# Graph network on one core: PSUM banks shared by several sums, later adds, and more rooms for gathered rows, planes and one-hots

## The chip, the cores and the metric

The kernel runs on one core of a Trainium2 chip. The metric is the device time of one launch in microseconds (us). TensorE (PE) does matrix products into PSUM, VectorE (DVE) and ScalarE (ACT) work element by element, GpSimd (POOL) issues the gathers by index, SyncE (SP) issues the plain transfers.

## What is computed

A graph of 6250 nodes with 128 features has 106250 edges (50000 drawn ones, each in both directions, and 6250 loops). Four networks follow one another, each with a residual and a layer norm:

```
x = layernorm(x + L0(x, edges, edge_attr))       # edge MLP, segment sum, GRU cell
x = layernorm(x + relu(conv(x)))                 # L1: normalised by degrees
x = layernorm(x + prelu(conv(x)))                # L2
h = relu(conv_w(x, W1)); h = relu(conv_w(h, W2)) # L3: weighted edges, 128 -> 256 -> 256
x = layernorm(x + conv_w(h, W3))                 #     -> 128

def _gcn_conv(x, W, b, src, dst, norm, n_nodes):
    m = x @ W
    msg = m[src] * norm[:, None]
    out = jax.ops.segment_sum(msg, dst, num_segments=n_nodes)
    return out + b
```

The change concerns the five products of a sparse 6250 x 6250 matrix with the rows of all nodes that L1, L2 and L3 need. They are the kernel's layers `l1`, `l2`, `l3a`, `l3b`, `l3c`. Layer `l3b` has rows of 256 features where the others have 128, as its product is taken between two weight matrices.

## The kernel before, in words

The first 2200 us (of the profile) run the edge network and the GRU cell and build the matrices in DRAM: blocks of 128 x 128 of counts (`counts_fwd`, `counts_rev`, for l1 and l2) or of weights (`weights_fwd`, for l3a to l3c). Nothing there changes.

`layer()` then makes each product in two ways at once. **Dense part:** the 49 node blocks form 13 groups of four. For most groups SP brings the group's matrix in seven chunks of 7 source blocks (`mat_...`, `slots` chunk slots), and PE multiplies every source block by it (L1469, out to `po_...`, four accumulators in PSUM). A little after its last chunk a group is taken: DVE adds what was left out (L1718) and for some groups a low sum (L1723), PE multiplies by the layer's weights (L1501 to L1523), and DVE and ACT finish the rows. The rows that fitted no block (the rest) come by one gather, L1376, and small matmuls L1417 and L1421 at the start of each layer.

**Low part:** the edges into the first few groups aren't multiplied as blocks. They are sorted by destination, and 69 *half steps* (103 in l3b) of four tiles of 128 edges each are woven into the dense part, so many to a chunk (`beside`), placed between the source blocks of a chunk. Half step j takes:

- POOL, `rows_of_step`: four gathers of 128 rows (L1390) into room j of a ring of `RL` rooms.
- DVE, `low_hots`: a one-hot of each edge's destination within 64 nodes (L1667), `HL` rooms, `HL - 1` half steps ahead.
- In l3a to l3c the rows are float32 and are made into three bfloat16 planes: ACT `high` (L1577, four operations, with the edge's weight), DVE `off_high` (L1675, four), ACT `mid` (L1583), DVE `last_plane` (L1681). There are two split rooms, so `high(j)` waits for PE's half step j-2. In l1 and l2 the table already has three planes.
- PE, the half step (L1440): 12 matmuls of 128 x 64 (24 in l3b) into one bank of PSUM.
- DVE, `add_sums` (L1690): that bank is added into `acc_...` at a place that is read from `low_first`.

The order is written out. At a chunk, DVE does for each of its half steps j: one-hots of j+3 (j+1 in l3b), `off_high(j+1)`, `add_sums(j)`, `last_plane(j+1)`. PE waits before half step j for its planes or rows, its one-hots, and for the bank:

```
if j >= pas:
    pe.wait_ge(added, j - pas + 1)
```

`pas` is the number of banks: 3, and 1 in l3b, which has only the bank `pl_l3b` for this. The rings lie in parts of the two large arrays `rows_a` and `rows_b` that a layer leaves free (`spare_of`), four rooms each and three in l3b.

Of the kernel before, what the change touches and what calls it, by code (L numbers as in the profile page):

```python
# [20 lines left out]
P = 128  # L21
N = 6250
E = 106250
FD = 128
# [8 lines left out]
TH = 4  # L33
# [88 lines left out]
def build(nc, a, out):  # L122
    with ExitStack() as ctx:
# [1050 lines left out]
        def layer(name, kind, K, Fo, given, mats, self_n, dis_in, bias, dis_out, wts, table, table_out, made, stored, slots,  # L1174
                  lows, spare):
# [16 lines left out]
            low_groups = list(range(low_n // GB))  # L1192

# [29 lines left out]
            if both:  # L1223
                for n, g in begun:
                    assert g * GB >= low_n or sum(len(js) for js in beside[:n]) >= min(low_js, PER_GROUP * g + LATE_BY)
            if not both:
                free = [p * CHKS + at for p in range(1, len(products) + 1) for at in LATER]
                for q in low_groups:
                    at = next(n for n in free if sum(len(js) for js in beside[:n]) >= min(low_js, PER_GROUP * q + LATE_BY))
                    free = [n for n in free if n > at]  # L1230
                    begun.append((at, q))
# [11 lines left out]
            RL = 3 if two else 4  # L1243
            HL = 2 if two else 4
            pas = 1 if two else 3

            with ExitStack() as c:
# [15 lines left out]
                room = spare[:, 0:RL * TH * wide] if exact else spare[:, 0:RL * TH * row_n // 2].bitcast(BF16)  # L1263
                ring = room.rearrange("p (q t f) -> p q t f", q=RL, t=TH)
                hot = sb(f"hot_{name}", [P, HL, TH, W], BF16, c)

                split = sb(f"split_{name}", [P, 2, 3, TH, wide], BF16, c) if exact else None
                rec_t = sb(f"rec_{name}", [P, 8], F32, c)
                near = sb(f"near_{name}", [P, 2], F32, c)
# [15 lines left out]
                pa = pl[:].unsqueeze(1) if two else ps(f"pa_{name}", [P, pas, 512], c)  # L1285
# [35 lines left out]
                def is_low(g):  # L1321

                    return g * GB < low_n

# [14 lines left out]
                with nc.Block() as block:  # L1339
# [25 lines left out]
                    def _(pool):  # L1365
# [19 lines left out]
                        def rows_of_step(j):  # L1385
# [3 lines left out]
                            for t in range(TH):  # L1389
                                pool.indirect_dma_start(  # L1390
                                    ring[:, j % RL, t, :], None, table,
# [12 lines left out]
                    def _(pe):  # L1404
# [23 lines left out]
                        def half_step(j):  # L1428
# [5 lines left out]
                            if j >= pas:  # L1434
                                pe.wait_ge(added, j - pas + 1)
                            for k in range(K):
                                for t in range(TH):
                                    for v in range(3):
                                        rows = split[:, j % 2, v, t, k * P:(k + 1) * P] if exact else ring[:, j % RL, t, v * P:(v + 1) * P]
                                        mm = nc.tensor.matmul(pa[:, j % pas, k * W:(k + 1) * W], rows, hot[:, j % HL, t, :],  # L1440
# [106 lines left out]
                    def _(act):  # L1547
# [23 lines left out]
                        def high(j):  # L1571

                            act.wait_ge(gathered[j % RL], 16 * TH * (j // RL + 1))
                            if j >= 2:
                                act.wait_ge(step_sum, j - 1)
                            for t in range(TH):
                                part = nc.scalar.activation(split[:, j % 2, 0, t, :], ring[:, j % RL, t, :], ACT.Copy,  # L1577
# [329 lines left out]
```

## Time and profile before

| | |
|---|---|
| runs of the kernel before | 4619.05 us median of 3 (4617.8 to 4621.76) |
| span of the one profiled execution | 5156.7 us |
| of it: up to layer l1 | 0 to 2200 |
| l1 | 2200 to 2778, 578 us |
| l2 | 2778 to 3250, 472 us |
| l3a | 3250 to 3771, 521 us |
| l3b | 3771 to 4637, 866 us |
| l3c | 4637 to 5157, 520 us |

No other time of the profiled execution is recorded than its span, which is 537.6 us longer than the median. Times within the profile are read against the span. In its rows the share in the last columns of a window is the granted clock of TensorE, then the share of DMA time and the rate; a value in square brackets in a timeline is the engine's idle time just before the row and what ended it.

### The profile page before, as it was taken

What the parts mean: (1) busy time and instruction counts of PE and PEld (TensorE: products, weight loads), DVE (VectorE), ACT (ScalarE), POOL (GpSimd) and SP (SyncE); (2) the same over time, 40 slices, a digit from 0 to 9 for tenths busy, and PEclk for the clock granted to TensorE, in tenths of its full rate; (3) what the DMA queues carried; (4) which work ended last, traced back from release to release, by engine and by line L of the source; (5) the groups of instructions that cost most, each with busy time, mean ns of one, the idle gap of its engine ahead of it and who ended that gap; (6) DMA issues with size and microseconds to landing.
All of it is one profiled execution on the core that took longest, in us unless ns stands there. A gap on an engine that the chain in (4) does not pass through costs nothing. (4 is left out here: it accounts for less than half of the span.)

```text
span 5156.7 us, 82749 instructions
## 1 busy us (share of the span) xinstructions
PE 4030.2 (78%) x30748; PEld 2679.0 (52%) x30767; DVE 3057.5 (59%) x6135; ACT 1489.2 (29%) x3024; POOL 2773.1 (54%) x2361
## 2 busy tenths in 40 slices
PE   2788788788888853268887888688978888887888
PEld 2677677677777743234443444344444554544344
DVE  5888777777787785835553233355435555522554
ACT  0333455455555531200000000122214433412332
POOL 3676666766776600046663665366436655605663
PEclk6777888898888876679998888799989999998999
DMA  4344566566666642079995666577745545537776
GB/s 148 116 125 131 183 194 201 182 213 198 198 204 199 206 137 81 29 253 318 318 325 173 196 204 191 188 274 276 284 149 187 184 159 182 179 115 246 267 264 232
DMA packets 611991, 1019.31 MB, mean 198 GB/s; under 512 B 90372, under 2 KB 417056, under 8 KB 611208
## 3 DMA queue, kind: packets, MB, share of 16 engines
q1 hardware_dynamic: 475788, 773.72, 44.0%
q0 software_dynamic: 90848, 199.74, 13.3%
q10 hardware_dynamic: 44956, 40.55, 2.4%
q8 instruction: 247, 4.05, 0.3%
q14 instruction: 152, 1.25, 0.1%
HBM read 736.98 MB, written 276.75 MB: 197 GB/s over the span
## 5 line engine op out<-in xcount | busy, mean ns | idle before, releaser
L871 POOL DMA_INDIRECT x<-p_table,src_i x832 | 1180.3, 1419 | 625.1 <-DVE x L610 338.3
L1390 POOL DMA_INDIRECT rows_b<-x_table,low_src x552 | 577.3, 1046 | 660.5 <-POOLq L140 309.8
L1390 POOL DMA_INDIRECT rows_a<-h_table,low_src x412 | 449.8, 1092 | 298.8 <-DVE split_l3b L1681 176.6
L1469 PE MATMUL po_l3b<-mat_l3b,rows_b 128*128 128x512 f32 (+1 forms) x1372 | 583.6, 573 | 29.0 <-DMA mat_l3b<-weights_fwd 20.6
L853 ACT CAST st_cnt<-ps_mat 128x512 bf16<-128x512 f32 (+1 forms) x825 | 445.4, 586 | 510.4 <-PE ps_deg L768 244.0
L783 PE MATMUL ps_mat<-rows_a,hot_s 128*128 128x128 bf16 x4851 | 406.2, 241 | 98.8 <-issue 68.4
L1469 PE MATMUL po_l3a<-mat_l3a,rows_a 128*128 128x512 f32 (+1 forms) x882 | 393.7, 593 | 46.6 <-DMA mat_l3a<-weights_fwd 32.1
L1469 PE MATMUL po_l3c<-mat_l3c,rows_a 128*128 128x512 f32 (+1 forms) x882 | 391.8, 591 | 28.1 <-DMA mat_l3c<-weights_fwd 19.3
L783 PEld LDWEIGHTS ps_mat<-rows_a,hot_s 128*128 128x128 bf16 x4851 | 327.1, 109 | 144.7 <-issue 88.6
L1469 PEld LDWEIGHTS po_l3b<-mat_l3b,rows_b 128*128 128x128 f32 x1372 | 250.4, 203 | 256.0 <-issue 233.5
L1469 PE MATMUL po_l<-mat_l,rows_b 128*128 128x512 bf16 (+1 forms) x1323 | 323.4, 394 | 64.5 <-issue 43.9
L1390 POOL DMA_INDIRECT rows_a<-x_table,low_src x276 | 281.2, 1019 | 168.6 <-issue 86.8
L1390 POOL DMA_INDIRECT rows_a<-m_table,low_src x276 | 277.2, 1004 | 170.2 <-issue 91.5
L1469 PE MATMUL po_l<-mat_l,rows_a 128*128 128x512 bf16 (+1 forms) x1323 | 296.7, 381 | 91.0 <-DVE mat_l L1709 70.4
L598 DVE TENSOR_TENSOR rows_a<-rows_a,slots 128x1792 bf16<-128x1792 bf16 (+1 forms) x198 | 366.7, 1885 | 1.4
L763 PE MATMUL ps_mat<-rows_a,hot_s 128*128 128x128 bf16 x1617 | 269.2, 232 | 110.3 <-ACT st_cnt L853 43.0
L766 PE MATMUL ps_mat<-hot_s,rows_a 128*128 128x256 bf16 x1225 | 338.2, 296 | 3.9 <-issue 3.9
L764 PE MATMUL ps_deg<-slots,hot_s 128*128 128x1 bf16 x2401 | 295.1, 172 | 50.3 <-issue 32.3
L858 ACT COPY st_wt<-ps_mat 128x512 f32<-128x512 f32 (+1 forms) x429 | 246.0, 573 | 159.8 <-PE ps_deg L768 59.7
L1624 ACT ACTIVATE t_l<-y_l 128x512 f32<-128x512 f32 (+1 forms) x26 | 15.7, 605 | 956.0 <-DVE y_l L1764 591.6
L793 PE MATMUL pm<-w1eT,rows_a 65*128 65x128 f32 x1664 | 270.1, 313 | 5.4 <-DVE x L610 4.6
L1469 PEld LDWEIGHTS po_l3a<-mat_l3a,rows_a 128*128 128x128 f32 x882 | 165.8, 206 | 201.9 <-issue 166.5
(407 smaller groups left out, 7488.0 us busy)
## 6 DMA issues: line engine op xcount, KB each, us to landing
weights_fwd<-st_wt SPq DMA_DIRECT2D x396, 256.0 KB
mat_l<-counts_fwd SPq DMA_DIRECT2D x112, 896.0 KB
mat_l3a<-weights_fwd SPq DMA_DIRECT2D x56, 1792.0 KB
mat_l3c<-weights_fwd SPq DMA_DIRECT2D x56, 1792.0 KB
counts_rev<-st_cnt SPq DMA_DIRECT2D x588, 128.0 KB
rev_l<-counts_rev SPq DMA_DIRECT2D x84, 896.0 KB
mat_l3b<-weights_fwd SPq DMA_DIRECT2D x42, 1792.0 KB
counts_fwd<-st_cnt SPq DMA_DIRECT2D x396, 128.0 KB
```

The lines of the kernel that those rows point to most:

```text
L598: V.tensor_tensor(hot_w[:, h, v, 0:n, :], hot_d[:, h, 0:n, :], per_row(slots[:, u % 2, 2 + v, ks], P), ALU.mult).then_inc(hots_ready, 1)
L763: nc.tensor.matmul(ps_mat[:, b, q * P:(q + 1) * P], half, rows, start=True, stop=True)
L764: nc.tensor.matmul(ps_deg[:, 2 * k + q:2 * k + q + 1], half, slots[:, u % 2, NV, k:k + 1], start=False, stop=False)
L766: nc.tensor.matmul(ps_mat[:, b, rev_at:rev_at + len(halves) * P], rows, hot_s[:, h, j0 + j, 0:len(halves) * P], start=True, stop=True)
L783: mm = nc.tensor.matmul(ps_mat[:, f % 3, (2 * j + q) * P:(2 * j + q + 1) * P], half, hot_w[:, h, v, j0 + j, :], start=(v == 0), stop=(v == 2))
L793: mm = nc.tensor.matmul(pm[:, j % 2, t * FD:(t + 1) * FD], edge[:, i % 2, (h * TH + t) * P:(h * TH + t + 1) * P], w1eT[:], start=True, sto ...
L853: nc.scalar.copy(st_cnt[:, q, :, j * 2 * P:j * 2 * P + n_col], ps_mat[:, f % 3, :].rearrange("p (d c) -> p d c", d=2)[:, :, 0:n_col]).then ...
L858: nc.scalar.copy(to, ps_mat[:, f % 3, 0:w]).then_inc(evicted, 1)
L871: pool.indirect_dma_start(ring[:, j % RING, t * FD:(t + 1) * FD], None, p_table, bass.IndirectOffsetOnAxis(src_i[:, j * TH + t:j * TH + t ...
L1390: pool.indirect_dma_start(ring[:, j % RL, t, :], None, table, bass.IndirectOffsetOnAxis(low_src[:, j * TH + t:j * TH + t + 1].bitcast(U32), 0)
L1469: mm = nc.tensor.matmul(po[:, p % 2, k, 0:nb * P].rearrange("p (d c) -> p d c", c=P), rows[:, s, k * P:(k + 1) * P], cols, start=(s == 0 a ...
L1624: nc.scalar.activation(t1[:, 0:nb, 0:FD], y2[:, f % ys, 0:nb], ACT.Square).then_inc(act_out, 1)
```

## The change

- **Banks.** In l1, l2, l3a and l3c the three banks hold two sums each (`SUMS` = 2, side by side in a bank). In l3b the one bank holds four. PE waits for adds only at the first sum of a bank, and then until all sums that lay in it are added; DVE adds a bank's sums only once its last sum is made (`in_full`).
- **Adds.** They come later in DVE's order: at half step j all adds up to j+1-`LAG` (3, and 1 in l3b), by whole banks, so in pairs, and in fours in l3b. The take of a low group first brings the adds up to what it needs (`needed`), and the chunk at which a low group may begin follows from that: the end of group 1 moves from chunk 33 to 38 in l3a and l3c, that of group 4 in l3b from 38 to 40.
- **Rooms.** One-hots: 8 rooms for 4, 3 for 2 in l3b, made as many half steps ahead as before. Ring: 8 for 4 in l2, 6 for 4 in l3a and l3c, as before in l1 (4) and l3b (3). Split rooms: 5 for 2 in l3c, 2 elsewhere. Chunk slots: 6 for 3 in l2. The small tile `near` now lies in `small`.

```diff
+            BANKS, SUMS, LAG = (1, 4, 1) if two else (3, 2, 3)
+            def in_full(j):
+                return min(low_js, -(-j // SUMS) * SUMS)
+            def needed(g):
+                return in_full(PER_GROUP * g + LATE_BY)
...
-            RL = 3 if two else 4
-            HL = 2 if two else 4
-            pas = 1 if two else 3
+            RL = len(ring_rooms)
+            HL, HOTS_AHEAD = (3, 1) if two else (8, 3)
+            SPLITS = 2 if two else 2 + len(split_rooms)
...
+                def sum_room(j):
+                    return pa[:, j // SUMS % BANKS, j % SUMS * K * W:(j % SUMS + 1) * K * W]
...
-                            if j >= pas:
-                                pe.wait_ge(added, j - pas + 1)
+                            if j % SUMS == 0 and j >= BANKS * SUMS:
+                                pe.wait_ge(added, j - BANKS * SUMS + SUMS)
+                            to = sum_room(j)
...
-                            if j >= 2:
-                                act.wait_ge(step_sum, j - 1)
+                            if j >= SPLITS:
+                                act.wait_ge(step_sum, j - SPLITS + 1)
...
+                        def add_until(end):
+                            while begun_adds[0] < end and in_full(begun_adds[0] + 1) <= end:
+                                add_sums(begun_adds[0])
+                                begun_adds[0] += 1
                         def add_sums(j):
...
-                            dve.wait_ge(step_sum, j + 1)
+                            dve.wait_ge(step_sum, in_full(j + 1))
...
                             g = tasks[f]
                             nb = blocks_in(g)
+                            if is_low(g):
+                                add_until(needed(g))
...
-                                if j + HL - 1 < low_js:
-                                    low_hots(j + HL - 1)
+                                if j + HOTS_AHEAD < low_js:
+                                    low_hots(j + HOTS_AHEAD)
                                 if exact and j + 1 < low_js:
                                     off_high(j + 1)
-                                add_sums(j)
+                                add_until(j + 1 - LAG)
                                 if exact and j + 1 < low_js:
                                     last_plane(j + 1)
...
-              tables[1], tables[2], rows_of(rows_a, FD), rows_of(rows_a, FD), 3, 0, spare_b)
+              tables[1], tables[2], rows_of(rows_a, FD), rows_of(rows_a, FD), 6, 0,
+              rooms_of(rows_b, a_end, b_end, step_planes) + rooms_of(rows_a, NP, a_end, step_planes), [])
...
-              m_table, None, None, None, 3, 0, spare_a)
+              m_table, None, None, None, 3, 0, rooms_of(rows_a, NP, a_end, step_rows),
+              rooms_of(rows_b, 0, 3 * step_planes, step_planes))
```

DVE in l3b, near the layer's start, before: from one-hots to one-hots is a half step, and each has its add (the three rows ahead of an add read where it goes).

```order
L1675 SCALAR_TENSOR_TENSOR rows_a<-rows_a,low_weight,split_l3b 128x256 x4
L1685 TENSOR_LOAD low_first
L1685 ISA x2
L1690 ISA
L1690 TENSOR_TENSOR acc_l3b<-acc_l3b,pl_l3b 128x2x64
L1681 TENSOR_TENSOR split_l3b<-rows_a,split_l3b 128x1024
L1667 TENSOR_TENSOR hot_l3b<-iota_row,low_local 128x256
L1675 SCALAR_TENSOR_TENSOR rows_a<-rows_a,low_weight,split_l3b 128x256 x4
```

The same engine and place after the change (L1683 is the one-hots, L1691 the subtractions, L1697 the last plane, L1712 the add).

```order
L1697 TENSOR_TENSOR split_l3b<-rows_a,split_l3b 128x1024
L1683 TENSOR_TENSOR hot_l3b<-iota_row,low_local 128x256
L1691 SCALAR_TENSOR_TENSOR rows_a<-rows_a,low_weight,split_l3b 128x256 x4
L1707 TENSOR_LOAD low_first
L1707 ISA x2
L1712 ISA
L1712 TENSOR_TENSOR acc_l3b<-acc_l3b,pl_l3b 128x2x64
L1707 TENSOR_LOAD low_first
L1707 ISA x2
L1712 ISA
L1712 TENSOR_TENSOR acc_l3b<-acc_l3b,pl_l3b 128x2x64
L1707 TENSOR_LOAD low_first
```

The four rows of an add stand four times in a row there, ahead of the last plane; the three half steps before have none.

POOL at the start of l2, before: the gathers of four half steps, then the loop's registers, then the rest's gather.

```order
L1390 DMA rows_b<-x_table,low_src 128x384 x16
L1341 TENSOR_LOAD left_i
L1341 ISA x2
L1342 TENSOR_LOAD left_i
L1342 ISA x2
L118 UNCONDITIONAL_BRANCH x2
L96 ISA
L1376 DMA sums_l<-x_table,rec_l 128x384
```

After (L1404 is the ring's gather, L1390 now the rest's):

```order
L1404 DMA rows_b<-x_table,low_src 128x384 x16
L1404 DMA rows_a<-x_table,low_src 128x384 x16
L1341 TENSOR_LOAD left_i
L1341 ISA x2
L1342 TENSOR_LOAD left_i
L1342 ISA x2
L118 UNCONDITIONAL_BRANCH x2
L96 ISA
L1390 DMA sums_l<-x_table,rec_l 128x384
```

The gathers of four more half steps, into rooms in the other array, stand ahead of the rest's gather.

## Rows read from the trace of the kernel before

**Rows 1.** The page's head.

```profile
span 5156.7 us, 82749 instructions
```

**Rows 2.** Windows by stage (3a, 3b, 3c): busy times, clock, DMA share, GB/s.

```profile
3250.00:3771.00 521.00, 440.99 (x1912) 226.59 (x1912) 231.10 (x569) 127.85 (x345) 282.17 (x277) 0.92 0.73 258
3771.00:4637.00 866.00, 755.61 (x4538) 434.76 (x4538) 434.59 (x815) 292.97 (x541) 450.72 (x413) 0.94 0.50 167
4637.00:5157.00 520.00, 425.60 (x1863) 211.89 (x1863) 242.31 (x647) 138.52 (x371) 278.18 (x277) 0.92 0.72 252
```

**Rows 3.** Groups by line and form, 3b: busy us, mean ns, idle before, releasers.

```profile
L1390 POOL DMA_INDIRECT rows_a<-h_table,low_src x412 | 449.8, 1092 | 298.8 <-DVE split_l3b L1681 176.6 <-issue 122.2
...
L1577 ACT ACTIVATE split_l3b<-rows_a,low_weight 128x256 bf16<-128x256 f32 x412 | 175.5, 496 | 268.6 <-DMA rows_a<-h_table,low_src 99.7 <-PE pl_l3b L1440 86.4 <-DMA rows_a<-x_table,low_src 73.5
...
L1681 DVE TENSOR_TENSOR split_l3b<-rows_a,split_l3b 128x1024 bf16<-128x1024 f32 x103 | 125.8, 1222 | 41.2 <-ACT split_l3b L1583 33.7 <-issue 7.4
...
L1440 PE MATMUL pl_l3b<-hot_l3b,split_l3b 128*128 128x64 bf16 x2472 | 91.5, 195 | 47.9 <-DVE split_l3b L1681 39.5 <-issue 8.1
...
L1690 DVE TENSOR_TENSOR acc_l3b<-acc_l3b,pl_l3b 128x128 f32 x103 | 29.4, 286 | 244.1 <-PE pl_l3b L1440 131.2 <-DMA rows_a<-x_table,low_src 112.8
...
L1718 DVE TENSOR_TENSOR sums_l3b<-po_l3b,left_l3b 128x1024 f32<-128x1024 f32 x12 | 14.7, 1221 | 45.0 <-PE po_l3b L1488 43.2 <-DMA rev_l<-counts_rev 1.8
```

**Rows 4.** Timeline of a half step in 3b: start, duration, engine, line, operation.

```profile
4035.68 0.86 PE L1440 MATMUL pl_l3b<-hot_l3b,split_l3b 128*128 128x64 bf16 x24 [0.47 <-issue]
...
4037.41 0.28 DVE L1690 TENSOR_TENSOR acc_l3b<-acc_l3b,pl_l3b 128x128 f32 x1
4037.53 1.04 ACT L1583 CAST split_l3b<-rows_a 128x1024 bf16<-128x1024 f32 x1 [1.78 <-DVE rows_a L1675]
...
4038.48 1.70 ACT L1577 ACTIVATE split_l3b<-rows_a,low_weight 128x256 bf16<-128x256 f32 x4
4038.60 1.23 DVE L1681 TENSOR_TENSOR split_l3b<-rows_a,split_l3b 128x1024 bf16<-128x1024 f32 x1 [0.91 <-ACT split_l3b L1583]
...
4039.93 0.86 PE L1440 MATMUL pl_l3b<-hot_l3b,split_l3b 128*128 128x64 bf16 x24
4040.21 1.67 DVE L1675 SCALAR_TENSOR_TENSOR rows_a<-rows_a,low_weight,split_l3b 128x256 f32<-128x256 f32 x4
```

**Rows 5.** Timeline of two adds close together, layer two.

```profile
2971.10 0.22 DVE L1690 TENSOR_TENSOR acc_l<-acc_l,pa_l 128x64 f32 x1 [3.52 <-DMA x<-p_table,src_i]
...
2971.96 0.22 DVE L1690 TENSOR_TENSOR acc_l<-acc_l,pa_l 128x64 f32 x1 [0.30 <-issue]
```

**Rows 6.** Timeline of a half step in 3c and what follows it.

```profile
4988.64 0.51 PE L1440 MATMUL pa_l3c<-hot_l3c,split_l3c 128*128 128x64 bf16 x12 [0.24 <-issue]
...
4998.40 0.40 ACT L1577 ACTIVATE split_l3c<-rows_a,low_weight 128x128 bf16<-128x128 f32 x1 [7.69 <-DMA rec_l3b<-left_rec]
...
4999.43 0.80 PE L1440 MATMUL pa_l3c<-hot_l3c,split_l3c 128*128 128x64 bf16 x12 [4.61 <-issue]
```

**Rows 7.** Windows of the same place.

```profile
4990.00:4998.80 8.80, 4.83 (x15) 2.03 (x13) 0.35 (x3) 1.02 (x3) 4.71 (x5) 1.00 0.41 143
4998.80:5002.20 3.40, 2.77 (x15) 1.76 (x16) 2.80 (x9) 2.19 (x7) 1.03 (x1) 0.50 0.80 243
```

**Rows 8.** Groups by line: PE's half steps in 3a and 3c, POOL's gathers in 3c.

```profile
L1440 PE MATMUL pa_l3a<-hot_l3a,split_l3a 128*128 128x64 bf16 x828 | 36.5, 195 | 37.5 <-issue 37.5
...
L1390 POOL DMA_INDIRECT rows_a<-m_table,low_src x276 | 277.2, 1004 | 170.2 <-issue 91.5 <-DVE split_l3c L1681 78.6
...
L1440 PE MATMUL pa_l3c<-hot_l3c,split_l3c 128*128 128x64 bf16 x828 | 37.4, 197 | 55.0 <-issue 55.0
```

**Rows 9.** Timeline of POOL at the start of 3c, after its first 20 gathers.

```profile
4692.41 1.17 POOL L1390 DMA_INDIRECT rows_a<-m_table,low_src  x1 [17.94 <-DVE split_l3c L1681]
```

**Rows 10.** Timeline of layer two's start: the rest's gather and PE's first rest matmuls.

```profile
2799.03 0.94 POOL L1376 DMA_INDIRECT sums_l<-x_table,rec_l  x1 [0.30 <-issue]
...
2812.25 0.48 PE L1421 MATMUL pl_l<-zero 128*128 128x128 f32 x2 [0.15 <-remote]
```

More of the change, by code:

```diff
@@ L1224, in layer @@
                 for n, g in begun:
-                    assert g * GB >= low_n or sum(len(js) for js in beside[:n]) >= min(low_js, PER_GROUP * g + LATE_BY)
+                    assert g * GB >= low_n or sum(len(js) for js in beside[:n]) >= needed(g)
             if not both:
@@ L1228, in layer @@
                 for q in low_groups:
-                    at = next(n for n in free if sum(len(js) for js in beside[:n]) >= min(low_js, PER_GROUP * q + LATE_BY))
+                    at = next(n for n in free if sum(len(js) for js in beside[:n]) >= needed(q))
                     free = [n for n in free if n > at]
@@ L1262, in layer @@
                 acc = sb(f"acc_{name}", [P, K, span + W], F32, c)
-                room = spare[:, 0:RL * TH * wide] if exact else spare[:, 0:RL * TH * row_n // 2].bitcast(BF16)
-                ring = room.rearrange("p (q t f) -> p q t f", q=RL, t=TH)
+                ring = [(room if exact else room.bitcast(BF16)).rearrange("p (t f) -> p t f", t=TH) for room in ring_rooms]
                 hot = sb(f"hot_{name}", [P, HL, TH, W], BF16, c)
-                split = sb(f"split_{name}", [P, 2, 3, TH, wide], BF16, c) if exact else None
+                split = [sb(f"split{q}_{name}", [P, 3, TH, wide], BF16, c)[:] for q in range(2)] if exact else []
+                split += [room.bitcast(BF16).rearrange("p (v t f) -> p v t f", v=3, t=TH) for room in split_rooms]
                 rec_t = sb(f"rec_{name}", [P, 8], F32, c)
-                near = sb(f"near_{name}", [P, 2], F32, c)
+                near = small[:, 0, 0:2]
                 kinds = 2 if both else 1
@@ L1283, in layer @@
                 pl = ps(f"pl_{name}", [P, 512], c)
-                pa = pl[:].unsqueeze(1) if two else ps(f"pa_{name}", [P, pas, 512], c)
+                pa = pl[:].unsqueeze(1) if two else ps(f"pa_{name}", [P, BANKS, 512], c)
                 mat_in = [sem(f"mat_in_{name}{q}") for q in range(slots)]
@@ L1438, in half_step @@
                                     for v in range(3):
[L1439 to L1440 removed]
+                                        rows = split[j % SPLITS][:, v, t, k * P:(k + 1) * P] if exact else ring[j % RL][:, t, v * P:(v + 1) * P]
+                                        mm = nc.tensor.matmul(to[:, k * W:(k + 1) * W], rows, hot[:, j % HL, t, :],
                                                               start=(t == 0 and v == 0), stop=(t == TH - 1 and v == 2))
@@ L1582, in mid @@
                             act.wait_ge(high_off, j + 1)
-                            nc.scalar.copy(split[:, j % 2, 1], ring[:, j % RL]).then_inc(mid_ready, 1)
+                            nc.scalar.copy(split[j % SPLITS][:, 1], ring[j % RL]).then_inc(mid_ready, 1)
                         def store(f):
@@ L1727, in take @@
                                 dve.wait_ge(taken, f + 1)
-                                dve.wait_ge(added, sum(len(js) for js in beside[:starts[f]]))
+                                dve.wait_ge(added, begun_adds[0])
                                 end = at + nb * P
@@ L1797, in _ @@
                         chain.step(V.memset(acc[:], 0.0))
-                        for j in range(HL - 1):
+                        for j in range(HOTS_AHEAD):
                             low_hots(j)
```

31 lines of the change are left out of this document (17 added, 14 removed).

## The prediction

> **What bounds the kernel now.** I read the page's head first: a span of 5156.7 us [rows 1]. The one profiled execution is 537.6 us (11.6%) longer than the median of the runs, 4619.05 us, so the sum below is made as a difference against the profiled execution and then added to the median. Terms that are chains of instruction durations carry over as they are; terms that are waits may belong to the profiled execution alone, and that doubt is a rival below. 0.2% (9 us) is about what a measurement of this kernel can tell from no change.
>
> The windows by stage [rows 2] come next. TensorE is busy for 441 of 521 us in 3a, 756 of 866 in 3b and 426 of 520 in 3c, and the DMA engines for 0.73, 0.50 and 0.72 of these stretches. So 3b goes by TensorE's program alone, and each microsecond that PE waits there is one of the kernel; 3a and 3c go by PE too, with the transfers close behind. Layer one keeps its rooms and chunk slots.
>
> In 3b the groups [rows 3] give most prices of a half step's parts: four gathers on POOL at 1.092 us, four high planes on ACT at 0.496, a last plane on DVE at 1.222 and an add at 0.286. PE idles 47.9 us before its 2472 small matmuls (103 half steps of 24), 39.5 of it for the last plane. The timeline of one half step after another [rows 4] shows the loop: PE ends half step j-1 at 4036.54; ACT's mid plane (1.04 us) ends at 4038.57 and the next high planes run 1.70 us from 4038.48; DVE's last plane from 4038.60 lets PE start half step j at 4039.93; and DVE's subtractions for j+1 start only at 4040.21 and take 1.67. The add of half step j-1 stood at 4037.41, **ahead** of all that.
>
> **3b: the add that PE waits for moves behind a step.** Before, the add of half step j-1 comes in DVE's step j-1, and PE's half step j waits for it; it is done 2.2 us early in the timeline. Now four sums lie in the one bank. The order shows three DVE steps without adds, then four adds in the step of j *behind* the subtractions of j+1, and PE's half step j (j a multiple of 4) waits for all four. DVE can't reach them sooner: the subtractions of j+1 wait for the high planes of j+1, and those for PE's half step j-1, since 3b still has two split rooms. From the end of PE's half step j-1: 0.3 us until ACT is through with the mid plane (ACT and DVE have caught up in the stall four steps before; in the timeline, with no such stall, it is 1.94), 1.70 for the high planes, 1.67 for the subtractions, then four adds. Two adds in a row stand 0.86 us apart and one lasts 0.22 there, 0.28 in 3b [rows 5, 4]: 3 x 0.86 + 0.28 = 2.86. Together 6.5, with hand-overs 6.6 us. PE's own work between half steps two source blocks apart is 3.39 us (4036.54 to 4039.93), so 5.1 for three and 6.8 for four. PE's order has 25 such waits: 16 at two blocks, 6 at three, 3 at four. Stalls: 16 x 3.2 = 51 and 6 x 1.5 = 9. Four of the waits lie in a chunk that also takes a group, where DVE has L1718 (1.221), L1723 of the same shape and a diagonal of half its width ahead: 4 x 3 = 12. **+72.** Upper end: 1.94 in place of 0.3 at 22 places, +36 more. Lower end: adds back to back at 0.28, 1.7 less at 22 places, -38.
>
> **The clock.** In 3c, after PE had stood for 4.61 us [rows 6], its granted clock was 0.50 for 3.4 us where it had been 1.00 [rows 7]: the lower of its two levels, 1.2 GHz; half speed for 3.4 us costs 1.7. The new stalls are shorter than that one. I take it for 20 of them and for 0.7 of these: **+24** (0 to 43, all 25).
>
> **3b, gain.** Three steps of four lose their add. Of the 47.9 us before half steps I take **-15** (0 to -48). The third one-hot room is worth 0: the last plane is the wait's releaser, not the one-hots, whose cover is that they are written a step ahead.
>
> **3a and 3c: six ring rooms for four, three banks of two sums for three of one, and in 3c five split rooms for two.** PE idles 37.5 and 55.0 us before their half steps, with no releaser named [rows 8]. More rooms let POOL and ACT run on while DVE is busy with a group's end, and at the layers' start: in 3c POOL stands 17.94 us once its rooms are full [rows 9]. But POOL is idle for 170.2 us of 3c in all, so gathers aren't late on the whole, and PE has dense matmuls to fill the time. I take a third of 92.5: **-30**. Ends: 0, and -120, all of the waits with a clock term of 1.7 at some 16 of them. The end of group 1 moves from chunk 33 to 38 in both, and group 4's in 3b from 38 to 40; the dense work between covers that: 0.
>
> **Layer two: eight ring rooms for four, six chunk slots for three.** POOL's order has 32 gathers ahead of the one at L1376 which the rest's sums need, where it had 16. L1376 starts at 2799.03, and 16 more gathers at 0.94 + 0.30 us put it at 2819; PE takes up the rest's sums at 2812.25 [rows 10]. PE would stand some 8 us, of which steps gathered sooner and more chunk slots give part back: **+5** (-10 to +20). Layer one: 0 (-10 to 0).
>
> **Sum:** +72 +24 -15 -30 +5 = +56, so 4619 + 56 = **4675 us**. This case's own range is 4637 (the adds at their lower end) to 4730 (the chain at its upper end, 36, and the clock at 43).
>
> **A rule that speaks against the sum.** In one place of 3c [rows 6] PE's half step ends at 4989.15, and ACT, whose high planes wait for it, starts at 4998.40 after 7.69 us idle. No full room explains that: PE had the only missing signal. So I count most of the 92.5 us as waits of the profiled execution. The Trainium skill (Trainium Kernel Development and Optimization, Best Practices) says that consistent bubbles can mean that SBUF or PSUM space has run out. By that rule the idle time before half steps is what this change removes, and the sum would be the first rival's. The same notes (Perfetto Trace Analysis, on an instruction's lifecycle) say that a semaphore update isn't part of the instruction's row; no run here shows yet how long one takes without the profiler.
>
> **Rivals.**
> *Full rooms were the limit (22%).* The idle before half steps is real in plain runs. For it: 37.5, 55.0 and 47.9 us stand before the same line in all three layers, and in 3c POOL does stop with its rooms full. Against it: [rows 6]. 0.8 x 92.5 goes (-74), the clock after 20 such stalls (-34), 3b's 47.9 goes (-48), and 3b's new stalls stay (+96): -60, **4559 us**.
> *Gathers set 3b's pace (14%).* Four gathers with their gaps are 4 x (1.092 + 0.30) = 5.57 us a half step, more than 3.39. If PE waits for gathers in a run of near half steps anyway, the stall is only 6.6 - 5.6 = 1.0 at 22 places and the takes' 12: +34, no clock term. The starts of 3a and 3c give 2 x 17.9 = 36 and their waits 10, 3b 15, layer two costs 5: -22, **4597 us**. Against it: group and timeline name the last plane, not a gather.
> *Little happens (8%).* The four adds are reached in time and the rooms were never short: **4612 to 4619 us**. Against it: the order puts the adds behind subtractions that can't start earlier.
> *The forecast (56%)* is the slower side's one mechanism. It decides as soon as the path from half step j-1 to the fourth add, 6.6 us, is longer than PE's work between.
>
> **How the numbers follow.** The forecast's 56 give 54 slower and 2 same; the first rival's 22 give 21 faster and 1 same; the second's 14 give 10, 2, and 2 slower; the third's 8 give 1, 6 and 1. Faster 0.32, same 0.11, slower 0.57. The range, 4575 to 4730, leaves out most of the first rival's lower part and the forecast's worst clock term.
>
> **What would show it.** Four adds in a row in 3b, about 0.86 us apart, and PE idle some 3 us before each fourth half step, ended by DVE's add; 3b 60 to 100 us longer than 866; more of 3b at 0.50 of the clock; 3a and 3c shorter by 10 to 20 us each; L1376's successor in layer two some 20 us behind the first gathers' end. It is wrong if the fourth add ends before PE arrives, or if 3b is no longer than before, or if the idle time before half steps in 3a and 3c is gone and the runs are faster by as much.

## The result, and the profile after

| | us |
|---|---|
| kernel before | 4620.41, median of 4 (4617.8 to 4626.03) |
| changed kernel | 4664.75, median of 4 (4659.21 to 4670.83) |
| ratio | 1.0096, 95% interval 1.0078 to 1.0114 |
| forecast | 4675, range 4575 to 4730 |

The change costs 44 us, 0.96%. That is slower, as forecast, and 10 us from the number. How its terms came out is told below.

First something without which no profile here can be read: the profile of before and the times above don't belong together. The changed kernel's profiled execution has a span of 4669.0 us and belongs to a run of 4670.83 us, where the profiled execution of before had 5156.7 [rows 1]. In the experiments the kernel before, unchanged, took 5169.8, 5169.88, 5109.26, 5112.47 and 5112.93 us on five chips, and 4620.07 on a sixth. So **chips come in two kinds** for this kernel, here called the quicker and the slower kind. (No chip was seen in both kinds. That each stays in its kind isn't shown.) By its span and its stages the profile of before is one of the slower kind; both medians of the result are of the quicker kind. The prediction took the difference for waits that belong to the profiled execution alone. They don't: on the slower kind profiled executions of the kernel before took 5168.13 and 5180.66 us, as long as the others there.

So the rows of before are answered below by two pages: the changed kernel, and the experiment h1, which on a quicker chip took 4625.75 us beside 4620.07 of the kernel before (ratio 1.0011, 0.9995 to 1.0028). h1 has 3b as before, the ring, split rooms and chunk slots of before, and elsewhere pairs of sums added in their own step. It stands in for the kernel before, of which no profile on a quicker chip exists and from which its time can't be told. Two things of the change are in h1 too and so in no difference below: the extra rooms for one-hots, and the pairs with the later start of group 1.

Windows by stage of h1 (layer two, 3a, 3b, 3c): length, busy times of PE, PEld, DVE, ACT, POOL, then clock, DMA share, GB/s.

```profile
2539.60:2937.90 398.30, 326.32 (x2354) 177.00 (x2354) 155.85 (x355) 10.53 (x26) 271.82 (x277) 0.93 0.69 219
2937.90:3389.50 451.60, 420.18 (x1912) 218.12 (x1912) 232.58 (x569) 128.68 (x345) 280.81 (x277) 0.97 0.84 297
3389.50:4192.90 803.40, 732.39 (x4538) 421.08 (x4538) 438.64 (x816) 291.22 (x541) 446.23 (x413) 0.97 0.53 180
4192.90:4625.60 432.70, 403.99 (x1863) 204.60 (x1863) 243.76 (x647) 139.27 (x371) 278.38 (x277) 0.97 0.86 303
```

The same windows of the changed kernel.

```profile
2546.70:2943.70 397.00, 322.37 (x2354) 176.59 (x2354) 154.96 (x355) 10.53 (x26) 272.79 (x277) 0.92 0.70 219
2943.70:3388.80 445.10, 419.52 (x1912) 219.37 (x1912) 234.49 (x569) 128.81 (x345) 281.44 (x277) 0.97 0.86 302
3388.80:4240.00 851.20, 749.65 (x4538) 426.30 (x4538) 443.09 (x815) 291.78 (x541) 433.67 (x413) 0.95 0.51 170
4240.00:4669.00 429.00, 402.67 (x1863) 205.38 (x1863) 245.45 (x647) 138.28 (x371) 278.18 (x277) 0.97 0.87 305
```

3b is 47.8 us longer. Layer two, 3a and 3c are 1.3, 6.5 and 3.7 us shorter, and layer one 3.0 (568.2 and 565.2). The layers together make +33; the other 10 us between the two spans lie before layer one (1971 and 1982 us), where the two programs are the same. That stretch scatters by itself: four executions on one chip of the slower kind took 2209 to 2239 us for it (f0 to f4 below).

What PE's idle time before half steps and before turns in 3b became, first in h1 and then in the changed kernel (groups by line and form; L1455 is the half step, L1528 the turn).

```profile
L1455 PE MATMUL pl_l3b<-hot_l3b,split_l3b 128*128 128x64 bf16 x2472 | 90.0, 194 | 22.5 <-issue 11.3 <-DVE split_l3b L1697 11.0
...
L1528 PE MATMUL pc_l3b<-ident,y_l3b 128*128 128x128 f32 x98 | 16.1, 315 | 31.0 <-DVE y_l3b L1776 31.0
```

```profile
L1455 PE MATMUL pl_l3b<-hot_l3b,split_l3b 128*128 128x64 bf16 x2472 | 94.1, 197 | 66.4 <-DVE acc_l3b L1712 62.8 <-DVE split_l3b L1697 3.5
...
L1528 PE MATMUL pc_l3b<-ident,y_l3b 128*128 128x128 f32 x98 | 14.2, 290 | 15.2 <-DVE y_l3b L1776 15.2
```

PE now waits 62.8 us for the add, a wait that did not exist. In return the 22.5 us for planes became 3.5, and the turns' 31.0 became 15.2: time that PE stands is time in which ACT and DVE catch up. In all, PE is idle for 101.6 us of 3b where h1 has 71.0 (a window's length less PE's busy time), 30.6 more. PE's busy time rose by 17.3 us (732.39 to 749.65) over the same 4538 instructions. 30.6 + 17.3 are the 47.8 us. The 17.3 go with the clock (0.97 to 0.95): by the clock's own records in the two traces, 3b of the changed kernel has 90.1 us at 0.50 and h1's has 49.0. The 41 us more at half speed would cost 20.5, an estimate, near the 17.3.

One stall, in the timeline of the changed kernel.

```profile
3451.73 0.86 PE L1455 MATMUL pl_l3b<-hot_l3b,split_l3b 128*128 128x64 bf16 x24
...
3452.87 1.70 ACT L1592 ACTIVATE split_l3b<-rows_a,low_weight 128x256 bf16<-128x256 f32 x4
...
3454.61 1.67 DVE L1691 SCALAR_TENSOR_TENSOR rows_a<-rows_a,low_weight,split_l3b 128x256 f32<-128x256 f32 x4
...
3456.19 0.71 DVE L1712 TENSOR_TENSOR acc_l3b<-acc_l3b,pl_l3b 128x128 f32 x2
...
3457.44 0.29 DVE L1712 TENSOR_TENSOR acc_l3b<-acc_l3b,pl_l3b 128x128 f32 x1 [0.54 <-DVE acc_l3b L1712]
...
3458.26 0.29 DVE L1712 TENSOR_TENSOR acc_l3b<-acc_l3b,pl_l3b 128x128 f32 x1 [0.53 <-DVE acc_l3b L1712]
...
3458.69 0.86 PE L1455 MATMUL pl_l3b<-hot_l3b,split_l3b 128*128 128x64 bf16 x24 [2.58 <-DVE acc_l3b L1712]
```

It is the loop of [rows 4] with the add moved. PE's half step ends at 3452.59, the high planes start 0.28 us later, the subtractions follow, and four adds end at 3458.55. PE stood 2.58 us. Windows of the changed kernel in and after that stall:

```profile
3456.00:3458.60 2.60, 0.11 (x1) 0.00 (x0) 1.40 (x6) 1.04 (x1) 1.89 (x2) 1.00 0.35 101
3459.70:3463.10 3.40, 3.40 (x6) 1.41 (x5) 1.99 (x5) 1.66 (x5) 2.78 (x3) 0.50 0.52 154
```

The granted clock falls to 0.50, the lower level, for 3.4 us after 2.6 us of an idle PE, as it did after a longer stop in [rows 7]. Not every wait has this behind it. Of the 20 waits for the add, 14 were followed by a stretch at 0.50, of 3.4 or 6.8 us. Of the ten that lasted 2.4 to 2.8 us, seven were. A wait of 3.35 us that ended at 4133.94 was not, as the window behind it shows:

```profile
4134.00:4140.00 6.00, 6.00 (x59) 3.50 (x60) 3.52 (x7) 2.75 (x5) 0.00 (x0) 1.00 0.05 5
```

3a and 3c after the change: PE's half steps (in 3c some planes lie in `rows_b`), which answer [rows 8].

```profile
L1455 PE MATMUL pa_l3a<-hot_l3a,split_l3a 128*128 128x64 bf16 x828 | 35.4, 193 | 0.2 <-issue 0.2
...
L1455 PE MATMUL pa_l3c<-hot_l3c,rows_b 128*128 128x64 bf16 x492 | 21.0, 193 | 0.2 <-issue 0.2
```

The 37.5 and 55.0 us of [rows 8] are gone. But on h1, on a quicker chip with the rooms of before, they are 5.9 and 4.4 us already:

```profile
L1455 PE MATMUL pa_l3a<-hot_l3a,split_l3a 128*128 128x64 bf16 x828 | 35.4, 193 | 5.9 <-DVE split_l3a L1697 4.4 <-issue 1.5
...
L1455 PE MATMUL pa_l3c<-hot_l3c,split_l3c 128*128 128x64 bf16 x828 | 35.4, 193 | 4.4 <-DVE split_l3c L1697 3.2 <-issue 1.2
```

Layer two: PE's wait for the rest's gather in h1 (sixteen gathers ahead) and PE's waits in its half steps.

```profile
L1455 PE MATMUL pa_l<-hot_l,rows_b 128*128 128x64 bf16 x828 | 36.3, 195 | 36.0 <-DMA rows_b<-x_table,low_src 16.2 <-issue 15.7 <-DVE hot_l L1683 4.0
...
L1431 PE MATMUL pl_l<-sums_l 128*128 128x128 bf16 x3 | 0.5, 304 | 9.7 <-DMA x<-p_table,src_i 9.7
```

The same in the changed kernel (thirty-two ahead; half steps from either array).

```profile
L1455 PE MATMUL pa_l<-hot_l,rows_b 128*128 128x64 bf16 x432 | 18.7, 194 | 9.7 <-issue 4.1 <-DMA rows_b<-x_table,low_src 2.8 <-DVE hot_l L1683 2.8
...
L1455 PE MATMUL pa_l<-hot_l,rows_a 128*128 128x64 bf16 x396 | 17.3, 195 | 10.3 <-DMA rows_a<-x_table,low_src 7.1 <-issue 3.2
...
L1431 PE MATMUL pl_l<-sums_l 128*128 128x128 bf16 x3 | 0.5, 305 | 28.7 <-remote 28.7
```

The wait for the rest's gather, which POOL now issues 40.2 us after its first (2587.06 and 2546.86), grew from 9.7 to 28.7 us, and half steps wait 20.0 us in place of 36.0. A new wait took the place of the ones removed. The six chunk slots changed little: PE's waits for the matrix are 17.9 us where h1 has 18.8.

### The profile page after: what moved, and what is told of

Its sections match the earlier page's. It is cut to its first block and busy times, and to the rows that moved or that the text cites. A ratio compares the mean times of both kernels' runs of the same rounds, so it can differ in the third digit from the quotient of the medians.

```text
span 4669.0 us, 82757 instructions
## 1 busy us (share of the span) xinstructions
PE 3827.6 (82%) x30767; PEld 2568.0 (55%) x30767; DVE 3072.3 (66%) x6135; ACT 1470.4 (31%) x3024; POOL 2802.3 (60%) x2361
## 3 DMA queue, kind: packets, MB, share of 16 engines
q14 instruction: 152, 1.25, 0.1%
## 5 line engine op out<-in xcount | busy, mean ns | idle before, releaser
L871 POOL DMA_INDIRECT x<-p_table,src_i x832 | 1214.4, 1460 | 398.3 <-issue 234.2
L1404 POOL DMA_INDIRECT rows_b<-x_table,low_src x420 | 460.0, 1095 | 538.8 <-POOLq L140 310.8
L1404 POOL DMA_INDIRECT rows_a<-h_table,low_src x412 | 432.7, 1050 | 299.0 <-DVE split_l3b L1697 180.4
L1484 PE MATMUL po_l3b<-mat_l3b,rows_b 128*128 128x512 f32 (+1 forms) x1372 | 586.9, 576 | 21.4 <-DMA mat_l3b<-weights_fwd 20.5
L1404 POOL DMA_INDIRECT rows_a<-x_table,low_src x408 | 410.6, 1006 | 127.9 <-issue 122.8
L1484 PE MATMUL po_l3a<-mat_l3a,rows_a 128*128 128x512 f32 (+1 forms) x882 | 376.5, 574 | 30.9 <-DMA mat_l3a<-weights_fwd 30.1
L783 PE MATMUL ps_mat<-rows_a,hot_s 128*128 128x128 bf16 x4851 | 360.6, 226 | 9.5
L1404 POOL DMA_INDIRECT rows_a<-m_table,low_src x276 | 277.2, 1004 | 87.7 <-issue 85.6
L763 PE MATMUL ps_mat<-rows_a,hot_s 128*128 128x128 bf16 x1617 | 254.7, 224 | 85.2 <-DVE rows_a L598 61.6
L766 PE MATMUL ps_mat<-hot_s,rows_a 128*128 128x256 bf16 x1225 | 321.2, 283 | 0.0
L783 PEld LDWEIGHTS ps_mat<-rows_a,hot_s 128*128 128x128 bf16 x4851 | 291.2, 101 | 48.0 <-ACT st_wt L858 37.9
L1484 PE MATMUL po_l<-mat_l,rows_b 128*128 128x512 bf16 (+1 forms) x1323 | 285.9, 371 | 18.7 <-DMA mat_l<-counts_fwd 17.9
L1639 ACT ACTIVATE t_l<-y_l 128x512 f32<-128x512 f32 (+1 forms) x26 | 15.7, 605 | 899.5 <-DVE y_l L1788 891.6
L1691 DVE SCALAR_TENSOR_TENSOR rows_a<-rows_a,low_weight,split_l3b 128x256 f32<-128x256 f32 x412 | 172.7, 481 | 156.0 <-ACT split_l3b L1592 154.4
```

The lines of the kernel that those rows point to most:

```text
L763: nc.tensor.matmul(ps_mat[:, b, q * P:(q + 1) * P], half, rows, start=True, stop=True)
L766: nc.tensor.matmul(ps_mat[:, b, rev_at:rev_at + len(halves) * P], rows, hot_s[:, h, j0 + j, 0:len(halves) * P], start=True, stop=True)
L783: mm = nc.tensor.matmul(ps_mat[:, f % 3, (2 * j + q) * P:(2 * j + q + 1) * P], half, hot_w[:, h, v, j0 + j, :], start=(v == 0), stop=(v == 2))
L871: pool.indirect_dma_start(ring[:, j % RING, t * FD:(t + 1) * FD], None, p_table, bass.IndirectOffsetOnAxis(src_i[:, j * TH + t:j * TH + t ...
L1404: pool.indirect_dma_start(ring[j % RL][:, t, :], None, table, bass.IndirectOffsetOnAxis(low_src[:, j * TH + t:j * TH + t + 1].bitcast(U32), 0)
L1484: mm = nc.tensor.matmul(po[:, p % 2, k, 0:nb * P].rearrange("p (d c) -> p d c", c=P), rows[:, s, k * P:(k + 1) * P], cols, start=(s == 0 a ...
```

## The experiments

Theory A is the prediction's: 3b's four adds behind the next step's subtractions cost the time, the rest moves little. Theory B: the waits of the first profile are real limits of the kernel, and 3b's stall only replaces them.

**e0, f0: the kernel before, again** (two chips, both of the slower kind). No edit.

> The kernel before, unchanged, for a second profile beside the changed kernel's, whose span (4669.0 us) is no longer than its runs. Theory A (3b's adds cost, rooms gain a little): the span comes out near 4620; 3b near 775 us where the changed kernel has 851, 3a and 3c some 455 and 440 (445 and 429 changed), PE hardly idle before half steps anywhere (under 15 us in a layer). Theory B (the waits of the first profile are real): the idle time before half steps is again 37, 48 and 55 us, and 3b is only some 40 us shorter than in the changed kernel.

> The kernel before once more. In the call above it took 5170 us, where it took 4620 beside the changed kernel, so chips differ. If this chip is of the quicker kind: Theory A: span near 4620, 3b near 775 us (851 in the changed kernel), 3a and 3c some 455 and 440, PE idle before half steps under 15 us in a layer. Theory B: 3b near 810 and idle time before half steps as in the first profile. On a chip of the slower kind: as e0, 5150 to 5190.

5168.13 and 5180.66 us, spans 5166.3 and 5178.9; e0's expectation had no room for that. Windows of f0 (layer two, 3a, 3b, 3c):

```profile
2792.00:3263.80 471.80, 368.00 (x2354) 188.87 (x2354) 154.55 (x354) 10.53 (x26) 271.20 (x277) 0.86 0.59 185
3263.80:3786.90 523.10, 442.75 (x1912) 227.00 (x1912) 230.81 (x569) 128.07 (x345) 281.05 (x277) 0.92 0.73 257
3786.90:4658.70 871.80, 760.31 (x4538) 435.52 (x4538) 434.79 (x816) 292.83 (x541) 446.09 (x413) 0.93 0.49 166
4658.70:5178.90 520.20, 427.03 (x1863) 211.63 (x1863) 242.25 (x647) 138.49 (x371) 275.97 (x277) 0.92 0.72 252
```

They repeat [rows 2] within 6 us, and the span includes every wait of the first profile in a run that took as long. On this kind of chip theory B's waits are real. On the other kind most of them are gone: h1 has 5.9, 22.5 and 4.4 us before half steps in 3a, 3b and 3c. What follows: a profile must be held against runs of the same chip before any of its waits is priced or dismissed.

**e1, f1: 3b's adds put back.**

```diff
-            BANKS, SUMS, LAG = (1, 4, 1) if two else (3, 2, 3)
+            BANKS, SUMS, LAG = (1, 1, 0) if two else (3, 2, 3)
```

> The changed kernel with 3b's adds put back: one sum to the bank, added in its own step. Theory A: the 62.8 us that PE waits for the add in 3b go, and with them stretches of low clock for 10 to 25 us: 4575 to 4595 us, 3b about 775. Theory B (PE then waits for the last plane instead, as in the first profile of before): 3b about 815, the kernel 4620 to 4635.

> The changed kernel with 3b's adds put back, as in e1. There 3b went from 928 us (e2) to 865, and the kernel from 5340 to 5273. On a chip of the quicker kind Theory A: the 62.8 us of waits go, 4575 to 4600 us, faster than before. Rival (rooms cost as on the slower kind, where 3a and 3c became 40 and 52 us longer): slower than before.

**e2, f2: the changed kernel, but layer two's rest gather after four half steps.**

```diff
-                        ahead = 0 if exact else RL
+                        ahead = 0 if exact else 4
```

> The changed kernel with four half steps' gathers ahead of the rest's gather in layer two, as before, the other four behind it. Theory A: L1390 comes 20 us earlier, PE's wait of 28.7 us before L1431 shrinks to about 9, the kernel 12 to 20 us shorter, 4645 to 4653. Rival: the transfers of the layer's matrix set the end of layer two, and the wait only moves: 4660 to 4670.

> The changed kernel with the rest's gather of layer two after four half steps. Theory A, quicker kind: the wait of 28.7 us before L1431 shrinks to about 9 and the kernel takes 4645 to 4653. Rival: the layer's transfers set its end and the wait only moves: 4660 to 4670. On the slower kind 5330 to 5345, as in e2.

**e3, i3: both edits.**

> Both edits in one. Theory A: they are in different layers, so the savings add: 4557 to 4580 us. If 3b's is not what I think, the sum of the two single differences tells.

> e3 once more, in the hope of a chip of the quicker kind: the changed kernel with 3b's adds put back and layer two's rest gather after four half steps. From the quicker kind's two profiles (h1 and the changed kernel): 3b 803 in place of 851, -48; PE's wait before L1431 9.7 in place of 28.7, -10 to -19; 3a and 3c stay at 445 and 429, 6.5 and 3.7 under h1. That is 4664.75 - 48 - 15 = 4600 us (4590 to 4615), 0.1 to 0.6% faster than before, and the rest of the rooms is worth that much on such a chip. Rival: layer two's end is set by PE's own work and waits elsewhere, and gives nothing: 4610 to 4620. On the slower kind: 5260 to 5280 beside 5170, or 2% over before.

All on chips of the slower kind (e on one, f on a second, i3 on a third); the column "before" is the kernel before on the same chip. The changed kernel itself was never run on this kind; e2 and f2 stand for it.

| | us | before | ratio (95%) | layer two, 3a, 3b, 3c |
|---|---|---|---|---|
| e1 | 5273.38 | 5169.8 | 1.0212 (1.0165 to 1.0258) | 483, 558, 865, 573 |
| e2 | 5339.86 | 5169.8 | 1.0337 (1.0298 to 1.0376) | 480, 559, 928, 573 |
| e3 | 5269.39 | 5169.8 | 1.0188 (1.0152 to 1.0225) | 479, 571, 870, 572 |
| f1 | 5279.63 | 5169.88 | 1.0235 (1.0186 to 1.0284) | 481, 569, 868, 573 |
| f2 | 5350.13 | 5169.88 | 1.0344 (1.0305 to 1.0384) | 479, 570, 937, 577 |
| i3 | 5210.79 | 5112.93 | 1.0196 (1.0171 to 1.0221) | 477, 549, 868, 567 |

Putting 3b's adds back gives 62 us of 3b from e2 to e1 and 69 from f2 to f1, and 66 and 71 us of the kernel; layer two's small edit differs there too. From e2 to e3, where 3b's edit is the only difference, it gives 57 us of 3b and 70 of the kernel. PE's half steps in 3b of f1 and then of f2:

```profile
L1455 PE MATMUL pl_l3b<-hot_l3b,split_l3b 128*128 128x64 bf16 x2472 | 92.3, 195 | 50.3 <-DVE split_l3b L1697 40.2 <-issue 9.9
```

```profile
L1455 PE MATMUL pl_l3b<-hot_l3b,split_l3b 128*128 128x64 bf16 x2472 | 101.0, 202 | 106.7 <-DVE acc_l3b L1712 89.4 <-DVE split_l3b L1697 12.1 <-issue 5.1
```

So 3b's part of theory A holds on this kind too. But with 3b undone the kernel is still 2.1 to 2.35% over before: here the other layers lose, 3a 40 to 53 us and 3c 51 to 57 in e1 to f2 (3a takes 518 and 523, 3c 520 and 520 in e0 and f0), where on the quicker kind they gain 6.5 and 3.7 against h1. Neither theory had that. The rest's gather is worth 2 to 4 us of layer two here (481 to 483 in e1 and f1 without the edit, 479 and 480 in e2, e3 and f2 with it); on the quicker kind, where it was expected to give 10 to 20, it was not measured, and neither was a kernel with 3b alone undone.

**f4: 3b keeps four sums to the bank, but adds them in the fourth one's own step.**

```diff
-            BANKS, SUMS, LAG = (1, 4, 1) if two else (3, 2, 3)
+            BANKS, SUMS, LAG = (1, 4, 0) if two else (3, 2, 3)
```

> 3b keeps four sums to the bank, but DVE adds the four in the step of the fourth (LAG 0), one step sooner and behind nothing that waits for high planes of the next. PE ends the fourth half step, four adds take 0.3 + 2.9 us, less than the 3.4 to the next: Theory A: PE's waits for the add fall from 63 to under 10 us, but the last plane now stands behind the four adds, which wait for PE: it ends 1.2 us later, so PE waits 1.0 to 1.3 at 16 to 22 places, some 20 to 25 us: 4600 to 4625 us on the quicker kind. If the place of the adds doesn't matter and their number does: as the changed kernel.

5352.49 us (ratio 1.0346, 1.0309 to 1.0383), the same as f2, which has layer two's small edit besides; but 3b takes 913.7 us, between f2's 937 and f1's 868. f4's time before layer one is 21 us longer than f2's (2239 and 2218), which hides it in the total. PE's half steps in 3b of f4:

```profile
L1455 PE MATMUL pl_l3b<-hot_l3b,split_l3b 128*128 128x64 bf16 x2472 | 94.9, 196 | 69.9 <-DVE split_l3b L1697 57.0 <-issue 12.7
...
L1528 PE MATMUL pc_l3b<-ident,y_l3b 128*128 128x128 f32 x98 | 20.1, 369 | 44.5 <-DVE y_l3b L1776 42.7 <-issue 1.7
```

The wait for the add is gone (89.4 to 0), as expected, and the last plane, now behind four adds that wait for PE, is what PE waits for: 57.0 us against f1's 40.2, and the turns 44.5 against 33.9. The place of the adds accounts for 23 of the 69 us. The other 46, twice what was expected, come with four sums in one bank: four adds in a bunch ahead of a last plane, and the later end of group 4 that goes with it. The two weren't told apart; the 57.0 us for the last plane speak for the bunch.

**g2: rooms only.** All sums as before, in all layers; rings, split rooms, one-hot rooms and chunk slots as changed.

```diff
-            BANKS, SUMS, LAG = (1, 4, 1) if two else (3, 2, 3)
+            BANKS, SUMS, LAG = (1, 1, 0) if two else (3, 1, 0)
```

> The changed kernel with all sums put back: 3b as before, and in the other layers one sum to a bank, added in its own step. What stays are the rooms: rings, split rooms, one-hots, chunk slots. On the slower kind of chip e1 left 3a at 558 to 569 us (before 518 to 523), 3c at 573 (before 520), layer two at 481 (468). If the later paired adds cost that: 3a near 520, 3c near 520, the kernel 5165 to 5195. If the rooms cost it: 3a 560 to 570, 3c 570, the kernel 5265 to 5285. On the quicker kind, if 3b's adds were the whole loss: 3b 770 to 790 us and the kernel 4575 to 4600; if rooms cost there too: 4630 or more.

**g3: banks only.** 3b as before, the other layers with pairs and late adds; rooms of before, except the one-hots.

```diff
-            BANKS, SUMS, LAG = (1, 4, 1) if two else (3, 2, 3)
+            BANKS, SUMS, LAG = (1, 1, 0) if two else (3, 2, 3)
...
-              tables[1], tables[2], rows_of(rows_a, FD), rows_of(rows_a, FD), 6, 0,
-              rooms_of(rows_b, a_end, b_end, step_planes) + rooms_of(rows_a, NP, a_end, step_planes), [])
+              tables[1], tables[2], rows_of(rows_a, FD), rows_of(rows_a, FD), 3, 0,
+              rooms_of(rows_b, a_end, b_end, step_planes), [])
```

(with `[:4]` on the rings of 3a and 3c, and no split rooms added in 3c).

> The other half of g2: 3b as before, layer two, 3a and 3c keep the paired sums and later adds, but have the rooms of before (ring of four, two split rooms, three chunk slots). One-hots keep eight rooms. g2 left 0.9% over before on the slower kind and 3a at 529, 3c at 524, where e1 had 558 to 569 and 573. If the later adds are what costs there: 3a 555 to 570, 3c 560 to 575, layer two near 470, the kernel 1.3 to 2.1% over before. If the two only cost together (POOL running further ahead of adds that come later): under 0.9%. On the quicker kind: 3b 770 to 790 us, the kernel within 0.5% of before.

Both on chips of the slower kind: g2 5154.92 beside 5109.26 (1.0088, 1.0066 to 1.0110), g3 5168.26 beside 5112.47 (1.0092, 1.0064 to 1.0120). Windows of 3a and 3c in g2:

```profile
3241.70:3770.60 528.90, 441.16 (x1912) 225.53 (x1912) 230.96 (x570) 127.97 (x345) 284.40 (x277) 0.91 0.73 254
...
4631.90:5155.90 524.00, 433.62 (x1863) 217.70 (x1863) 240.32 (x647) 134.89 (x371) 275.30 (x277) 0.89 0.72 250
```

and in g3:

```profile
3218.30:3771.70 553.40, 452.55 (x1912) 231.29 (x1912) 233.91 (x569) 127.82 (x345) 278.11 (x277) 0.91 0.70 243
...
4625.90:5168.30 542.40, 438.27 (x1863) 218.12 (x1863) 245.02 (x647) 138.18 (x371) 275.86 (x277) 0.89 0.69 242
```

On the slower kind each half costs 0.9% by itself, and 0.88 + 0.92 = 1.8 is near the 1.9 to 2.35% of the kernels that have both. In 3a and 3c g3's half, the pairs, late adds and the later start of group 1, looks like the larger part (553 and 542 against 529 and 524). But g2 and g3 ran on two chips, and the kernel before has no profile on either. PE's half steps in 3a of g2, the kernel with six ring rooms:

```profile
L1455 PE MATMUL pa_l3a<-hot_l3a,split_l3a 128*128 128x64 bf16 x828 | 36.2, 195 | 32.5 <-issue 32.5
```

f0 has 35.3 us there with four rooms and e0 31.8, so six rooms took nothing of it that can be told from scatter.

**What the rooms cost on the slower kind, at layer two's start.** The traces show one such place. PE has 147 small matmuls there while POOL issues its first gathers. Changed kernel, quicker chip:

```profile
2549.34 11.15 PE L1484 MATMUL po_l<-mat_l,rows_b 128*128 128x128 bf16 x147 [17.88 <-DMA mat_l<-counts_fwd]
```

f1, slower chip, PE and POOL near the end of the same stretch:

```profile
2821.79 0.26 PE L1484 MATMUL po_l<-mat_l,rows_b 128*128 128x128 bf16 x1 [2.54 <-issue]
2824.59 0.26 PE L1484 MATMUL po_l<-mat_l,rows_b 128*128 128x128 bf16 x1 [2.54 <-issue]
...
2821.70 0.95 POOL L1404 DMA_INDIRECT rows_a<-x_table,low_src  x1 [0.30 <-issue]
```

PE gets one matmul off and then stands for 2.54 us with nothing waited for, while gathers are issued every 1.25 us. POOL's last gather there starts at 2827.96, and from 2834.41 PE's matmuls run without a stop. On the slower kind the 147 matmuls take 28.6 to 31.1 us where 16 gathers stand ahead of the rest's (the first profile, e0, f0, g3) and 49.2 to 50.5 where 32 do (e1, f1, f4, g2). With 16, the rest's and 16 more (e2, e3, f2, i3) they take 45.1 to 48.4, so bringing the rest's gather forward could give little. On the quicker kind they take 12.2 us in h1 and 11.2 in the changed kernel, whose 32 gathers cost PE nothing there. So on the slower kind 16 more gathers early hold PE up some 20 us. Layer two as a whole is 13 to 17 us longer in e1 to e3 than in e0 (466), and 7 to 9 in f1 and f2 than in f0 (472). Why gathers hold PE up on these chips and not on others is open.

**h1: g3 with the pairs added in their own step.**

```diff
-            BANKS, SUMS, LAG = (1, 1, 0) if two else (3, 2, 3)
+            BANKS, SUMS, LAG = (1, 1, 0) if two else (3, 2, 0)
```

> g3 with the pairs of sums added in the step of the second one (LAG 0) instead of two steps later; rooms as before, 3b as before. g3 was 0.9% over the kernel before, 3a at 553 and 3c at 542. If the lateness of the adds costs that on the slower kind: 3a 520 to 530, 3c 520 to 528, the kernel 0 to 0.3% over before. If it is the pairing (or the later start of group 1, which comes with it): 3a 545 to 560, 3c 540 to 550, 0.7 to 1.1% over. On a chip of the quicker kind both give 3b 770 to 790 and the kernel within 0.5% of before.

This one ran on a quicker chip: 4625.75 us beside 4620.07, 1.0011 (0.9995 to 1.0028). 3b takes 803 us, above the 770 to 790 expected: the waits for planes (22.5) and turns (31.0) are there on this kind too. Against the changed kernel's 851 it prices 3b's adds, as shown above. It says nothing on whether pairing, lateness or the later start of group 1 costs the slower kind its 3a and 3c; that stays open.

## Why the prediction was right, and where it was not

**Right, by its main step.** The wait that moves behind a step, in 3b, is the loss. The parts of the chain hold one by one: high planes 0.28 us after the half step's end (0.3 forecast), 1.70, 1.67, adds in a bunch, 20 waits put down to the add where the order has 25. The stall at two source blocks is 2.58 us rather than 3.2, since the first two adds stand 0.42 us apart (two in 0.71) and only the later ones 0.82: the chain takes 5.96 us, not 6.6. Forecast for the adds +72, measured 62.8.

**The clock.** +24 forecast, from a fall after 14 of 20 stalls; PE's busy time rose by 17.3. The fall came after 14 of 20, as it happened. But six of the low stretches lasted 6.8 us and not 3.4, and 3b of h1 has 49.0 us at 0.50 without any of these waits, part of it behind the waits for planes and turns that the change shortened. So the size is near by two errors of opposite sign.

**The turns' waits, left out of the sum, and the gain of 15, undersized.** Half steps' other waits fell by 19 us (22.5 to 3.5), near the 15 of the sum, which was taken from the 47.9 us of a slower chip. The turns' waits, which had no term in the sum, fell by 15.8. A stall that is put into a loop lets the engines behind it catch up, so part of it is time that PE would have waited a little later. 3b in all: +81 forecast (72 + 24 - 15), +47.8 measured.

**3a and 3c, -30 forecast, -10.2 measured, and for a wrong reason.** The step that failed is "I count most of the 92.5 us as waits of the profiled execution". They were waits of the chip: on the slower kind every run has them, and on the quicker kind h1 has 5.9 and 4.4. A third of 92.5 had no ground. The two rows of h1 would have given 10, and 10.2 came, against h1; what pairs are worth against the kernel before isn't in it. The rule named in the prediction, that consistent bubbles can mean that buffers ran out (the Trainium skill, Trainium Kernel Development and Optimization, Best Practices), would have had the 92.5 us go. On the kind of chip that has these bubbles, six ring rooms left 32.5 us in 3a where four had 31.8 and 35.3, so there they don't come from a full ring. On the quicker kind 10.2 us of layers went with idle time of 10, which agrees with it.

**Layer two, +5 forecast, -1.3 measured.** The wait at the rest's sums grew by 19.0 us, near the upper bound of 20 and far from the 8 of the argument, which took PE's arrival from a slower chip, where the gathers hold PE up (2812.25 in [rows 10], 34 us into the layer; in the changed kernel PE arrives 15 us into it). The half steps' waits fell by 16.0 and PE's busy time by 4.0.

**The sum.** Forecast +56, measured +44.3: 3b 33 too high, 3a, 3c and layer two together 13 too low (-25 forecast, -11.5 measured), layer one 3 off, and 10 us before layer one that the trace of h1 does not have, where the code is the same. Without those 10 the layers make +33, which is further from the forecast than the +44.3 is. The number came as near as it did because the errors have opposite signs; that part is luck.

**The rivals.** *Full rooms were the limit* falls on both kinds: the kernel is slower on both. *Gathers set 3b's pace* falls: PE's waits name planes and adds, and in the changed 3b POOL waits for the last plane for 180.4 us. On the slower kind the change costs 3.4% (f2, with layer two's small edit), which lies outside the range: no case of the prediction had 3a and 3c lose.

**A version that beats both** was not found. e3 and i3 are 1.9% over before on the slower kind. On the quicker kind the same kernel should come to about 4600 us (4664.75, less 47.8 for 3b and up to 19 for the rest's gather), an estimate that no run backs.

## What to carry to other kernels

When sums share a bank, the wait for the bank covers all of them: ask where on the adding engine the **last** add of the bank stands, and what that engine must wait for ahead of it. If that path leads back to the very engine that waits for the bank, the add should come ahead of it. And adds in a bunch hold up what stands behind them: f4 has them in their own step and 3b is still 46 us longer than with single sums. Rooms bought against a wait were worth that wait here and no more, and a prologue sized by the number of rooms delays whatever stands behind it in the queue. Hold a profile's span against runs of the same chip before calling its waits real or false.

## What the runs showed of the hardware

- The kernel before takes 4602 to 4631 us on one chip (13 runs) and 5068 to 5189 on five others. No chip was seen in both kinds.
- The slower kind is longer in every stage, also before layer one (2211 us in f0, 1971 in h1) and in 3a (523 in f0, 452 in h1), with a DMA share of 0.73 against 0.84 for the same bytes. It isn't longer once a layer's half steps and their gathers are over: from PE's last half step to the layer's end 3a takes 50.0 us and 3c 46.3 in both f0 and h1. What makes a chip so is open.
- On the slower kind PE stands at "issue", with nothing waited for, mostly while gathers go: in f0 for 75.9 us of layer two, 75.4 of them within 3.5 us of the start of a gather, and in f1 for 84.0 us of 3c, 80.0 of them so (0.88 and 0.70 of these layers lie within 3.5 us of one). h1 has 15.7 and 1.2 us of it there.
- One change can have either sign in the same layer: against h1, 3a and 3c gain 6.5 and 3.7 us on the quicker kind; against the kernel before, they lose 40 to 53 and 51 to 57 on the slower.
- Waits of PE of 2.4 to 2.8 us were followed by the lower clock level seven times in ten, and one of 3.35 us was not. 3b of the changed kernel has 90.1 us at 0.50 of the clock where h1 has 49.0, and PE's busy time is 17.3 us longer.
